# Deformable convolution: corners summed on VectorE, turned in 32x32 blocks, and multiplied for six or seven tiles at once

## The reference, cut to what matters

```python
def _L3_conv_ref(x, offset_w, deform_w):
    offset = _conv2d(x, offset_w)             # 2*9 channels: (dy, dx) of each tap
    patches = _deform_patches(x, offset)      # [B, C, 9, H, W]
    wk = deform_w.reshape(Cout, C, 9)
    y = jnp.einsum('bckhw,ock->bohw', patches, wk)
    avg = jnp.mean(y, axis=(2, 3), keepdims=True)
    std = jnp.std(y, axis=(2, 3), keepdims=True, ddof=1)
    return y * jax.nn.sigmoid(avg + std)

def _deform_patches(x, offset):               # sy, sx: the moved position of a tap
    y0, x0 = floor(sy), floor(sx); ly, lx = sy - y0, sx - x0
    p = corner(y0i, x0i, (1 - ly) * (1 - lx))     # a pixel of x (0 outside) times a weight
    p = p + corner(y0i, x0i + 1, (1 - ly) * lx)
    p = p + corner(y0i + 1, x0i, ly * (1 - lx))
    p = p + corner(y0i + 1, x0i + 1, ly * lx)
    return p
```

## Time and profile before

| | |
|---|---|
| median of 3 runs | 14692.38 us (14690.25 to 14722.44) |
| the profiled execution | 14656.86 us |
| its span | 14654.9 us |
| busy: PE / PEld | 56% / 39% of the span |
| busy: DVE | 45% |
| busy: ACT | 20% |
| busy: POOL | 51% |
| granted TensorE clock, mean | 0.739 |

### The profile page before, as it was taken

How to read it: one execution, slowest core, us unless ns; L and a number is a source line. 1 busy time by engine, 2 the same in 40 slices (tenths; PEclk the granted TensorE clock), 3 DMA queues, 4 the chain that set the end, 5 groups by cost and what they waited for, 6 DMA issues and landing times.

```text
span 14654.9 us, 154001 instructions
## 1 busy us (share of the span) xinstructions
PE 8240.4 (56%) x51639; PEld 5651.9 (39%) x51639; DVE 6540.2 (45%) x13232; ACT 2973.2 (20%) x5102; POOL 7483.2 (51%) x7657
## 2 busy tenths in 40 slices
PE   6887888889453535444454535354444545353533
PEld 2333444449343433333333434343333333343433
DVE  5655555553235343434344353434343443534343
ACT  3433444433111111111111111111111111111111
POOL 0011222222366666666566666666666666666665
PEclk9998899999676767666676767666666767676766
DMA  3322111117333333333333333333333333333332
GB/s 91 88 81 71 53 57 53 61 47 228 100 97 110 99 107 102 113 94 113 98 107 110 97 108 97 109 103 112 94 113 95 113 109 98 109 97 106 103 96 83
DMA packets 503966, 1436.58 MB, mean 98 GB/s; under 512 B 128981, under 2 KB 234197, under 8 KB 474577
## 3 DMA queue, kind: packets, MB, share of 16 engines
q0 software_dynamic: 353344, 970.88, 22.5%
q1 hardware_dynamic: 150032, 458.00, 10.4%
HBM read 1175.46 MB, written 252.90 MB: 97 GB/s over the span
## 4 chain that ended last, share of the span: by engine, by line
another core or an unknown queue 38%; PE 16%; issue 12%; DVE 3%; ACT 3%; POOL 2%; DMA 0%; ACTq 0%; DVEq 0%; POOLq 0%; SPq 0%
PE e_ps L1939 9%; PE e_ps L1930 3%; POOL e_g L1783 2%; ACT e_corners L1846 2%; PE e_ps L1878 1%; PE e_ps L1889 1%; PE e_ps L1904 1%; DVE e_sty L2099 1%; DVE e_g L2090 1%; DVE e_g L2092 1%; DVE e_big L2112 0%; DVE e_x3t L1964 0%; DMA e_g<-table_dram,e_index_slots 0%; ACT e_pad L1820 0%
## 5 line engine op out<-in xcount | busy, mean ns | idle before, releaser
L1783 POOL DMA_INDIRECT e_g<-table_dram,e_index_slots x7056 | 6787.9, 962 | 4077.6 <-issue 2012.1
L1939 PE MATMUL e_ps<-e_corners,e_w_def 128*64 128x128 f32 x14112 | 2585.5, 358 | 4504.9 <-ACT e_corners L1846 3118.6
L1939 PEld LDWEIGHTS e_ps<-e_corners,e_w_def 128*64 128x64 f32 x14112 | 2280.0, 187 | 4790.6 <-ACT e_corners L1846 3282.8
L1930 PE MATMUL e_ps<-k_ident,e_g 128*128 128x128 f32 x7056 | 1281.1, 327 | 1263.0 <-DVE e_g L2092 654.7
L1846 ACT ACTIVATE e_corners<-e_ps 128x512 f32<-128x512 f32 (+1 forms) x2352 | 1027.0, 489 | 3253.4 <-remote 2383.7
L2060 DVE COPY e_index_slots<-e_index_now 128x9 uint32<-128x9 uint32 x784 | 141.3, 181 | 3272.9 <-DMA e_g<-table_dram,e_index_slots 3222.1
L1930 PEld LDWEIGHTS e_ps<-k_ident,e_g 128*128 128x128 f32 x7056 | 969.2, 168 | 1585.1 <-issue 899.5
L2089 DVE TENSOR_TENSOR e_ps<-e_g,e_ps 128x512 f32<-128x512 f32 (+1 forms) x2352 | 1327.0, 564 | 120.9 <-DMA e_g<-table_dram,e_index_slots 58.5
L1852 ACT ACTIVATE e_big<-e_ps 64x128 f32<-64x128 f32 x784 | 212.6, 271 | 5706.3 <-remote 4282.0
L2092 DVE TENSOR_TENSOR e_g<-e_g,e_ps 128x512 f32<-128x512 f32 (+1 forms) x2352 | 1301.1, 553 | 110.7 <-remote 12.2
L2090 DVE TENSOR_TENSOR e_g<-e_g,e_ps 128x512 f32<-128x512 f32 (+1 forms) x2352 | 1283.6, 546 | 0.0
(11 more groups left out here) (438 smaller groups left out, 8421.3 us busy)
## 6 DMA issues: line engine op xcount, KB each, us to landing
e_g<-table_dram,e_index_slots POOLq DMA_INDIRECT x7056
table_dram<-e_rt SPq DMA_DIRECT2D x32, 1624.0 KB
a_xt<-x_in SPq DMA_DIRECT2D x16, 1568.0 KB
v_dram<-a_vout SPq DMA_DIRECT2D x32, 784.0 KB, 8.5
b_xt<-v_dram SPq DMA_DIRECT2D x16, 1568.0 KB
v_dram<-b_vout SPq DMA_DIRECT2D x32, 784.0 KB, 7.7
c_v2t<-v_dram SPq DMA_DIRECT2D x16, 1568.0 KB
c_xt<-x_in SPq DMA_DIRECT2D x16, 1568.0 KB, 6.5
```

The source lines that it names most:

```text
L1783: pool.indirect_dma_start(out=g[:, slot, tap * CORNERS:(tap + 1) * CORNERS], out_offset=None, in_=table, in_offset=bass.IndirectOffsetOnAx ...
L1930: mm = pe.transpose(ps[:, TURN[tap // 4], (tap % 4) * P:(tap % 4 + 1) * P], g[:, slot, tap * CORNERS:tap * CORNERS + 2 * C], k.ident[:, :])
L1939: mm = pe.matmul(ps[0:C, OUT, 0:P], w_d[:, tap, :], corners[:, tap, :], start=(tap == 0), stop=(tap == TAPS - 1))
```

## The change

**Sums and turning.** The nine transpositions on PE and the three copies on ACT are gone. DVE now multiplies all left corners of a tile in one operation of 9 x 128, and then in three batches of three taps multiplies the right corners (384) and adds in three operations of 192 the upper pair, the lower pair and the two sums. One operation (`dve.transpose`) then turns the tile's 128 pixels x 9 x 64 sums in blocks of 32 x 32 and writes them into `turned`: there the partitions 32q to 32q+31 hold 32 channels of the pixels 32q to 32q+31 of the tile (a quarter), in 18 steps (nine taps x two halves of the channels), with the pixels along the free axis. `turned` has two buffers.

**Products.** The 49 tiles are cut into eight blocks of 7 and 6 (`BOUNDS`). For a block PE runs 18 steps x 4 quarters: matmuls of 32 rows, 128 columns of weights (the 64 output channels twice) and 224 or 192 pixels, each quarter into a bank of its own. ACT copies these four banks into `big`, which is now 128 partitions (both images) x 3136.

**Waits and order.** POOL waits for `summed`, which DVE's transposition counts up, where it waited for `bank_done`. `turned` is guarded by `out_done`: DVE starts a block when the one two before it is multiplied. The columns, the offsets and the turning of the offsets of the next pair stand as one piece each in front of blocks 2, 3 and 4, with a ring of six PSUM banks (`RING`) in place of two, and the means in front of block 1. `finish` of pair p is cut in three parts and runs on DVE behind tiles 4, 5 and 6 of pair p + 1, with 7 operations for the statistics in place of 14 and one on `big` in place of two, each on 128 partitions; x3 comes back and the result leaves in one DMA each. The first and the last pair are written out, the loop runs over the 14 others.

**Memory.** The constants that only earlier phases use go into a scope that is closed before the deform phase, and the array `w3_def` is laid out anew (32 rows four times, 18 steps x 128).

```diff
-        TURN, OUT, PREP, HALF, WEIGHTS = (0, 1, 2), 3, (4, 5), 6, 7
+        OUT, PREP, HALF, WEIGHTS = (0, 1, 2, 3), (4, 5), 6, 7
         SMALL = PREP[1]
-        BATCHES = ((0, 4), (4, 8), (8, TAPS))
+        RING = PREP + OUT
...
-                        pool.wait_ge(bank_done, (r - 1) * (3 * SLOTS) + (3 * slot + 3))
+                        pool.wait_ge(summed, (r - 1) * SLOTS + (slot + 1))
...
+                def block_products(p, n):
+                    lo, hi = BLOCKS[n]
+                    wide = (hi - lo) * QUARTER
+                    pe.wait_ge(summed, p * PX_TILES + hi)
+                    need(pe, out_ready, p * len(BLOCKS) + n)
+                    for step_ in range(TAPS * 2):
+                        for q in range(4):
+                            rows = slice(q * QUARTER, (q + 1) * QUARTER)
+                            mm = pe.matmul(ps[:, OUT[q], 0:wide], w_d[rows, step_, :], turned[rows, n % 2, step_, 0:wide],
+                                           start=(step_ == 0), stop=(step_ == TAPS * 2 - 1))
                     mm.then_inc(out_done, 1)
...
+                def pair(p, ahead):
+                    for n in range(len(BLOCKS)):
+                        if ahead is not None:
+                            if n == MEANS_BLOCK:
+                                means(ahead)
+                            elif n == ROWS_BLOCK:
+                                pe.wait_ge(out_ready, p * len(BLOCKS) + n)
+                                columns(ahead)
+                            elif n == OFFSETS_BLOCK:
+                                pe.wait_ge(out_ready, p * len(BLOCKS) + n)
+                                offsets(ahead)
+                            elif n == TURN_BLOCK:
+                                turn_offsets(ahead)
...
+                        block_products(p, n)
...
-                        dve.tensor_tensor(left, left, spread(0), ALU.mult).then_inc(weighted, 1)
-                        dve.wait_ge(weighted, t * 6 + (2 * n + 2))
-                        dve.tensor_tensor(left, left, half, ALU.add).then_inc(added, 1)
...
+                    dve.tensor_tensor(left, left, spread(0, TAPS, 0), ALU.mult).then_inc(weighted, 1)
+                    for n, (a, b) in enumerate(BATCHES):
+
+                        upper, lower = left[:, a:b, 0, :], left[:, a:b, 1, :]
+                        half = ps[:, HALF, 0:(b - a) * 2 * C].rearrange("p (k n c) -> p k n c", n=2, c=C)
                         need(dve, added, t * 3 + n)
...
+                        dve.tensor_tensor(half, sides[:, a:b, 1, :, :], spread(a, b, 1), ALU.mult).then_inc(weighted, 1)
+                        dve.wait_ge(weighted, t * 4 + (n + 2))
+                        dve.tensor_tensor(upper, upper, half[:, :, 0, :], ALU.add).then_inc(joined, 1)
+                        dve.tensor_tensor(half[:, :, 1, :], lower, half[:, :, 1, :], ALU.add).then_inc(joined, 1)
+                        dve.wait_ge(joined, t * 6 + (2 * n + 2))
+                        dve.tensor_tensor(upper, upper, half[:, :, 1, :], ALU.add).then_inc(added, 1)
+                    dve.wait_ge(added, t * 3 + 3)
+                    to = turned[:, block % 2, :, (at_tile - lo) * QUARTER:(at_tile - lo + 1) * QUARTER]
+                    dve.transpose(to.rearrange("p (k h) x -> p k h x", h=2),
+                                  left[:, :, 0, :].rearrange("p k (h x) -> p k h x", x=QUARTER)).then_inc(summed, 1)
...
+                def pair(p, behind, ahead):
+                    for at_tile in range(PX_TILES):
+                        turn(p, at_tile, ahead is None)
+                        if behind is not None and FINISH_AT <= at_tile < FINISH_AT + 3:
+                            finish(behind, at_tile - FINISH_AT)
+                        if ahead is not None:
+                            between(ahead, at_tile)
+                    if ahead is not None:
+                        switch(ahead)
```

365 lines of the change are left out of this document (177 added, 188 removed).

## The result

| | before | after |
|---|---|---|
| median | 14704.29 us | 15077.45 us |
| lowest to highest | 14690.25 to 14722.44 | 15069.06 to 15086.82 |
| ratio to before | | 1.0253, 95% interval 1.0235 to 1.0271 |
| the profiled execution's span | 14654.9 us | 15067.1 us |

The account below looks back on a forecast made before the run. POOL's gathers wait for slots that PE, its signals late, releases; without those pauses 3874 start + 8940 gathers + 31 stretching + 46 end = 12,891 us of span, scaled to 12,925 us; range 12,840 to 13,450.

Parts of the forecast that it names:

- Rival A: Deform stage: DVE's transposition holds POOL's gathers up, +118 to +329 us, 13,040 to 13,255 us; chance 0.14.
- a term of 31: `finish` in the next pair: its operation on `big` stretches a gather from 0.95 to 3.03 us, 31 us in all.
- Slots are released by DVE: Gather loop waits for DVE instead of PE; DVE's tile of 7.2 us stays under POOL's 11.4.
- Products in blocks: PE's matmuls take 14 us a block; products up to some 60 us hide behind the gathers, at no cost.
- the tightest place: DVE's start of block 5 (tile 31) after block 3: 76 us or twice that against 137 us, costed at nothing.
- Rival B: Deform stage: late signals stay on the path and make POOL pause; 13,030 to 13,750 us, chance 0.18.
- the likely place: Before tile 31: four late signals of 27 us follow each other, POOL pauses up to 55 us a pair, +825 us.
- Rival D: Data cannot follow uninterrupted gathers, or DVE needs over 11.4 us a tile; 13,100 us up, 13,700 taken; chance 0.06.
- Rival C: PE's row groups in the products do not overlap: 77 us a block, PE bounds, 15,550 us; chance 0.04.
- Slower: Whole kernel: slower than before by more than about 0.2% (29 us); chance 0.04.
- The end: After the last gather: last sums, products, copies and statistics, 46 us with signals.

Follow-up runs that it names:

- dve11: The changed kernel with DVE's sums in two batches of six and three taps, 11 instructions a tile instead of 15; 15,039 us, 1.023 of the kernel before.
- corner6: The changed kernel with sums taken corner by corner on DVE, 38 instructions and 6 semaphore updates a tile; 14,664 us, 1.001 of the kernel before.
- nopro: The changed kernel with 8 instead of 72 product matmuls a block on PE (output wrong); 14,500 us, 0.986 of the kernel before.
- fewpe11: The `dve11` kernel with 8 product matmuls a block and 14 matmuls each for columns and offsets (output wrong); 14,019 us, 0.957 of the kernel before.
- rest3: The changed kernel with POOL waiting for its gathered data to land behind slots 1, 3 and 6; 14,935 us, 1.018 of the kernel before.

## Why the prediction was wrong, point by point

**Right.** What bounds the kernel before, as far as it was said: POOL waits for slots that PE releases late. The durations: transposition 0.778 us (0.77), the multiplications 1.34 and 0.56 (1.37 and 0.56), the additions 0.355 (0.36), the tile unhindered 7.0 us (7.2). Products of a block without gathers beside them, 6.1 to 10.2 us (14): the row groups overlap. Rival A did not happen: the gathers' mean is 965 ns. First gather at 3857 us (3874).

**Small terms.** The prediction counted 1.267 us a gather, where the steps are 1.25; so it put the pauses before at 1796 us, 120 less than the 1916 above. The single operation on `big` (L2086) stretched the gather beside it to 4.18 us, and not to the 3.03 of its like: 15 x 3.2 = 49 us for a term of 31.

**The step that failed** is the one behind "Slots are released by DVE": "What is late next is POOL itself, if DVE is faster than 11.4 us a tile." It took DVE's tile as the sum of its operations. That holds only where no gathers crowd it. Beside uninterrupted gathers a tile is 15 instructions x 1.40 us = 21.0, nearly twice POOL's 11.3, and the change had raised DVE's instructions from 10 a tile (nine and the index copy) to 15. Before, DVE hardly met this: it lost 110.7 us before all its additions, after 2314. The trace before has a mean stretch of 18 gathers between pauses, after has 30. That PE stopped POOL first is my reading of it. What this step cost by itself is less clear than that it failed: `dve11` cut the crowded tile to 15.4 us and gained next to nothing, and `corner6` lengthened it and was faster by 2.4%.

**The second one** is in "Products in blocks" and in the tightest place: 14 us a block, and an excess "covered by filled slots", costed at nothing. It is the one that runs price: thinning PE's work took 577 us off (`nopro`), and with that of the preparation 1020 us (`fewpe11` against `dve11`). PE's own instructions are late, not its signals alone. Block 0 took 72 us in the mean (up to 98), block 6 took 81, and while columns and offsets crept, blocks 2 and 3 began 98 and 122 us after their sums (means of the loop's 14 pairs). DVE stood still for 30 us at tiles 25 and 31 each.

**Rival B** had the nearest cause and the right side of the forecast, at a chance of 0.18. Its price, +825 us at most in the likely place, counted four late signals of 27 us at one place of a pair. DVE stands still mainly at eight places (tiles 0, 5, 13, 19, 25, 31, 35 and 37) and inside a good third of its tiles, and POOL pauses 2322 us in all. What it lacked was already in the trace before, in a stretch that I had not looked at. PE, the second batch of four transpositions of one tile, 14 us after POOL had resumed at 4059.95:

```profile
4074.09 0.34 PE L1930 MATMUL e_ps<-k_ident,e_g 128*128 128x128 f32 x1 [1.78 <-issue]
4076.22 0.37 PE L1930 MATMUL e_ps<-k_ident,e_g 128*128 128x128 f32 x1 [1.79 <-issue]
4078.32 0.37 PE L1930 MATMUL e_ps<-k_ident,e_g 128*128 128x128 f32 x1 [1.73 <-issue]
4080.41 0.37 PE L1930 MATMUL e_ps<-k_ident,e_g 128*128 128x128 f32 x1 [1.73 <-issue]
```

These records of one batch lie 2.1 us apart, though nothing stands between them; at 4063.68, 3.7 us after POOL had resumed, nine of them took 1.30 us together. So it is PE's instructions that come late, and not just their signals. I read 33.29 us of ACT's idleness as late signals of PE, and so thought that fewer signals would do.

**Rival D** came near the truth in a part of its condition ("DVE needs more than 11.4 us"): in crowded stretches DVE does, in the mean it needs 10.5, and for another reason than the transposition; its 13,700 us was 1400 too low. **Rival C** was nearest in the number, 15,550 us, and its 77 us a block is what blocks 0 and 6 took; but that is luck, since the overlap which it denied took place. "Slower" stood at 0.04. What argued against D, 38 gathers without a pause, was true of POOL and told nothing of the engines beside it.

**The end** cost 68 us instead of 46: at the last gather DVE was six tiles behind, and those run at 6.9 us each.

**Where the expected gain went.** The pauses (1916 us by the count used here) were to vanish. In their place came 2322 us: through DVE's own lateness (its tiles stretch by 2755 us in all) and through PE's (1811 us before the index copies, where DVE mostly stands at the guard), of which the seven slots hide a part. How the 2322 us divide between the two is open; removing most of PE's work takes away some 1000 of them.

**Open.** Through what the engines' completions pass, and why gathers hold it, no run shows. One rival was not tried: that the recording of the executions takes part. Every run here comes with a recorded span and granted clock, so none without a recording is at hand to compare with, and a step of 1.40 us for each instruction, whether or not it updates a semaphore, would fit a cost of writing records too. The times stand as measured; that the same happens without a recording is not shown. Why the kernel before, with more instructions in all (154,001 against 148,082), ends with 400 us less of pauses is not settled either. What differs is that its work comes evenly, tile by tile; `corner6`, whose DVE stops POOL every two tiles, also comes to 1904 us. That both have short stretches fits, and `rest3` with stretches as short (18 gathers in the mean) and 2178 us speaks against it.

## What to carry to other kernels

Before taking a slower engine off the release of a buffer, ask what the faster producer will do to the rest once nothing stops it: look in the trace for the longest uninterrupted run of that producer, and read there how far apart the others' instructions lie, those that wait for nothing above all. Durations of single operations did not tell an engine's pace beside these gathers; the number of its instructions told how long a crowded tile of DVE is. It did not tell the kernel's time (`dve11` with fewer and `corner6` with more both went against that), so a count is a warning and no forecast. And a run that rests the producer behind every step is a cheap first experiment: it shows whether the others are slow by themselves.
